# Work of a later layer moved from the setup of an attention stage into its first eleven steps

## Chip, cores and metric

One core of a Trainium2 chip runs the whole program. The metric is the device time in microseconds, the median of several executions.

## What is computed

Two decoder layers on `x` of 8 x 256 tokens by 256 features, in float32. Layer 0: attention with 16 heads of 128, cross attention with linear feature maps to a context of 8 x 64 tokens, and a gated feed-forward part whose weights are first rounded to a 4-bit table (NF4) in blocks of 64. Layer 1: an attention over features, a gated cross attention to the same context ("memory"), and a feed-forward part with ternary weights. Cut to the parts that the change touches:

```python
x = x + attn(layernorm(x), w_qkv, w_o)             # 16 heads, causal mask absent
# values are scaled by the column sums of the softmax: out = einsum('bhqk,bhkd->bhkd', probs, v)
k = (memory_tokens @ wk.T); v = (memory_tokens @ wv.T)   # layer 1, memory: keys and values of the context
scalers_1 = max(abs(blocks), axis=1)               # NF4: one maximum for each block of 64 weights
# the scalers are centred by their mean, rounded to 8 bits per group of 32, and put back
w1 = ternary_quantize(c_fc); w2 = ternary_quantize(c_proj)   # scale = mean(abs(w))
```

## The kernel before

`attention_part` runs the first attention and, beside it, prepares everything of the later parts that depends on weights or on the context alone. `streams_part` then runs the rest over the eight sequences; the change does not touch it.

**Setup.** SyncE issues the loads in program order. TensorE transposes the normalised tokens (16 tiles, `transpose_tokens`), makes the keys and values of the context for layer 0 (`keys`, line 952, and line 1005), and the keys for layer 1 into banks 6 and 7 (`keys(bank[6:8], wk1, ...)`, copied by ACT at line 520). Then a loop over t = 0 to 15 mixes, on TensorE, the transposes of tile t + 4, at even t a feature product (`key_features`, line 967), at t = 4, 8, 12 and at the end a sum of features and values (`key_values`, line 989, "kv sum"), and at t = 1, 5, 9, 13 the memory values of layer 1 (`memory_values`, line 978, copied by ACT at line 545). VectorE in the same loop makes the statistics of four tiles at t = 1 and 5, normalises tile t + 6, splits tile t + 4 into two halves of 16 bits (`xn_lo`, line 676), evicts the feature product (line 728), and at t = 4, 6, 8 takes a third of the block maxima (`block_max`, line 693). At t = 15 it takes their reciprocal (line 736). TensorE then makes the first product of value and output weights (`value_out(0)`), waits for ACT's copy of the last kv sum, and starts the steps.

**Steps.** There are 64 steps, four for each head, each on two sequences: 11 written out, then a loop of eight steps six times, then the last ones. In step i TensorE computes queries and keys of step i (lines 74 to 76), the scores of step i - 1 (line 1064), the update of step i - 2 and its column sums (lines 1091 and 1093). The scores have one pair of banks, so those of step i - 1 wait until ACT has made the exponentials of step i - 2 (line 580); these wait for VectorE's row maximum (line 853). The column sums wait for VectorE's reciprocals (lines 840, 842), which POOL splits. `m_ps` is bank 6, used by `value_out` for each head at the step i = 4, 8, ... (`later_head(i, c, 0)`).

Behind its work for a step VectorE does one-time work, in the order of the code: `block_sums` at i = 0, `scale_codes` (12 instructions in a chain, lines 745 to 768) at i = 2, sums of the ternary weights (line 892) at i = 3 and 4, lin maxima at i = 1, maxima of kv0 (line 906) at i = 5, the ternary scales at i = 6, `linear_scales` at i = 9. At i = 2, 6, 10 it makes the scales of the next head (`scales`, lines 633 to 646) ahead of the row maximum. At i = 10 it waits for `rep_in`, the block scales repeated by column.

**SyncE's queue** is written out by hand; a wait in it holds back all that follows. `absmax_to_all` sends the maxima of a head's weights through memory to all partitions (write, wait, read), `load_prepared` waits for the split of an earlier head and loads a head's weights. The block maxima go out in five small transfers (line 389) and come back by rows (line 391) for `block_sums`.

## Time and profile before

| | |
|---|---|
| median of 3 runs | 932.9 us (932.67 to 932.92) |
| profiled execution, its own time | 934.24 us |
| its span (first to last instruction) | 932.4 us |
| TensorE busy | 858.7 us (92%) |
| VectorE busy | 729.2 us (78%) |
| ACT busy | 520.5 us (56%) |
| POOL busy | 369.0 us (40%) |
| mean granted TensorE clock | 0.98 |

PE is TensorE, PEld its weight loads, DVE VectorE, SPq the queue of SyncE. The granted clock is a share of 2.4 GHz; 0.50 is its lower level of 1.2 GHz. A row of the timeline gives start and length in us, the engine, the line, the operation, the tile written and those read, the shape, how many instructions are merged, and in brackets the idle time before and what ended it. Busy shares are means over stages with different limits, so the stages are read one by one.

### The profile page before, as it was taken

The numbers are of one execution on the slowest core, as the hardware profiler recorded it, in microseconds if no ns is written. First come the engines' busy times: TensorE is split into PE (matmuls) and PEld (weight loads), VectorE is DVE, ScalarE is ACT, GpSimd is POOL, SyncE is SP. The second block draws the span as 40 slices with busy tenths as digits, with TensorE's granted clock in tenths as the row PEclk, the third lists the DMA queues.
The fourth block names the chain that finished last, engine by engine and source line by source line (L and its number), as shares of the span: only waits on it lengthen the run. The fifth ranks groups of instructions, "written<-read, shape, count | busy, mean of one in ns | idle before, by whom it ended". The sixth has DMA issues, their size and how long they took to land. (4 is left out here: it accounts for less than half of the span.)

```text
span 932.4 us, 18697 instructions
## 1 busy us (share of the span) xinstructions
PE 858.7 (92%) x6868; PEld 637.5 (68%) x6868; DVE 729.2 (78%) x1777; ACT 520.5 (56%) x1245; POOL 369.0 (40%) x356
## 2 busy tenths in 40 slices
PE   4798998999999999999999986999988889999786
PEld 3455766777777777777777765787856568777554
DVE  5738867878888788887887745898798879887895
ACT  1435576656665566656665643554364863535556
POOL 3104455545555555545554553044133031522410
PEclk9889999999999999999999997999999999999999
DMA  9022331011101111011100000000000010000001
GB/s 285 32 65 68 55 93 35 2 35 34 34 7 27 34 34 34 0 34 34 34 5 6 1 1 1 1 2 1 1 2 1 1 46 2 1 1 1 1 1 46
DMA packets 34722, 25.56 MB, mean 27 GB/s; under 512 B 9492, under 2 KB 31596, under 8 KB 34668
## 3 DMA queue, kind: packets, MB, share of 16 engines
q1 hardware_dynamic: 34380, 24.56, 10.1%
q8 instruction: 35, 0.57, 0.3%
q10 hardware_dynamic: 288, 0.26, 0.1%
q14 instruction: 19, 0.16, 0.1%
HBM read 22.65 MB, written 2.17 MB: 27 GB/s over the span
## 5 line engine op out<-in xcount | busy, mean ns | idle before, releaser
L476 POOL CAST exp_hi<-exp_scores 128x1024 f16<-128x1024 f32 x64 | 67.0, 1047 | 217.9 <-ACT exp_scores L580 217.9
L74 PE MATMUL banks<-value_out_hi,xn_t_hi 128*128 128x256 f16 x512 | 140.8, 275 | 2.3 <-DVE X L874 2.3
L478 POOL TENSOR_TENSOR exp_lo<-exp_scores,exp_hi 128x1024 f16<-128x1024 f32 x64 | 140.7, 2198 | 5.1
L580 ACT ACTIVATE exp_scores<-banks,exp_bias,unscale 128x256 f32<-128x256 f32 x256 | 141.0, 560 | 2.1
L75 PE MATMUL banks<-value_out_lo,xn_t_hi 128*128 128x256 f16 x512 | 140.6, 275 | 0.0
L76 PE MATMUL banks<-value_out_hi,xn_t_lo 128*128 128x256 f16 x512 | 140.6, 275 | 0.0
L1064 PE MATMUL banks<-qk 128*128 128x256 f32 x512 | 122.7, 383 | 9.9 <-ACT exp_scores L580 9.9
L1064 PEld LDWEIGHTS banks<-qk 128*128 128x128 f32 x512 | 97.2, 191 | 31.4 <-issue 10.5
L874 DVE SCALAR_TENSOR_TENSOR X<-banks,colsum,X 128x256 f32<-128x256 f32 x256 | 106.2, 477 | 11.0 <-DVE colsum L865 9.6
L562 ACT ACTIVATE qk<-banks 128x512 f32<-128x512 f32 x128 | 75.8, 601 | 59.1 <-PE banks L76 59.1
L853 DVE TENSOR_REDUCE neg_rowmax<-banks 128x4 f32<-128x1024 f32 x64 | 78.1, 1221 | 31.4 <-PE banks L1064 31.4
L74 PE MATMUL banks<-xn_t_hi,head_weights_hi 128*128 128x512 f16 x256 | 96.9, 378 | 0.6 <-issue 0.6
L76 PE MATMUL banks<-xn_t_hi,head_weights_lo 128*128 128x512 f16 x256 | 97.0, 379 | 0.0
L75 PE MATMUL banks<-xn_t_lo,head_weights_hi 128*128 128x512 f16 x256 | 96.9, 379 | 0.0
L1282 POOL TENSOR_TENSOR rstd_stream<-rstd_stream,neg_half 128x2 f32<-128x2 f32 x40 | 29.2, 732 | 150.4 <-DVE rstd_stream L1430 139.2
L576 ACT ACTIVATE exp_bias<-neg_rowmax,unscale 128x4 f32<-128x4 f32 x64 | 18.8, 294 | 101.8 <-DVE neg_rowmax L853 101.8
L75 PEld LDWEIGHTS banks<-value_out_lo,xn_t_hi 128*128 128x128 f16 x512 | 50.5, 99 | 12.3 <-issue 0.3
L74 PEld LDWEIGHTS banks<-value_out_hi,xn_t_hi 128*128 128x128 f16 x512 | 50.5, 99 | 11.4 <-DVE X L874 4.4
L76 PEld LDWEIGHTS banks<-value_out_hi,xn_t_lo 128*128 128x128 f16 x512 | 50.5, 99 | 6.2
L1293 POOL TENSOR_TENSOR big_stream<-big_stream,den_stream 128x1024 f32<-128x1024 f32 x16 | 30.3, 1901 | 61.2 <-DVE den_stream L1546 61.2
L435 POOL TENSOR_TENSOR head_weights_lo<-head_weights,head_weights_hi 128x512 f16<-128x512 f32 x32 | 38.7, 1212 | 32.1 <-ACT head_weights_hi L494 32.1
L580 ACT ACTIVATION_READ_ACCUMULATOR exp_scores<-banks,exp_bias,unscale 128x1 f32 x256 | 50.8, 198 | 0.0
(238 smaller groups left out, 1965.9 us busy)
## 6 DMA issues: line engine op xcount, KB each, us to landing
head_weights<-in_wqkv_d SPq DMA_DIRECT2D x32, 128.0 KB, 3.7
weight_absmax_rows<-across_partitions SPq DMA_DIRECT2D x15, 256.0 KB, 4.1
X<-in_x_d SPq DMA_DIRECT2D x4, 512.0 KB, 7.5
head_weights<-in_wqkvt_d SPq DMA_DIRECT2D x16, 128.0 KB, 3.4
head_weights<-in_w_o_d SPq DMA_DIRECT2D x16, 128.0 KB, 3.5
out<-X SPq DMA_DIRECT2D x8, 256.0 KB, 2.1
res_then_ternary_then_kv<-in_c_fc_d SPq DMA_DIRECT2D x1, 1024.0 KB, 6.5
res_then_ternary_then_kv<-in_c_proj_d SPq DMA_DIRECT2D x1, 1024.0 KB, 8.2
```

The source lines that it names most:

```text
L74: nc.tensor.matmul(out, lhs[0], rhs[0], start=first, stop=False)
L75: nc.tensor.matmul(out, lhs[0], rhs[1], start=False, stop=False)
L76: return nc.tensor.matmul(out, lhs[1], rhs[0], start=False, stop=last)
L435: nc.gpsimd.tensor_tensor(wlo[:, u, 2 * a:2 * a + 2], wst[:, u, 2 * a:2 * a + 2], whi[:, u, 2 * a:2 * a + 2], ALU.subtract).then_inc(wlo_r ...
L476: nc.gpsimd.tensor_copy(probh[:, s1_.par], prob[:, s1_.par]).then_inc(exph_ready, 1)
L478: nc.gpsimd.tensor_tensor(probl[:, s1_.par], prob[:, s1_.par], probh[:, s1_.par], ALU.subtract).then_inc(expl_ready, 1)
L562: nc.scalar.activation(qk[:, st.par, s, :], qk_ps[s], ACT.Copy).then_inc(qk_ready, 1)
L580: last = nc.scalar.activation(prob[:, s1_.par, t, :], sc_ps[t // ST][:, t % ST, :], ACT.Exp, bias=nbias[:, t:t + 1], scale=unscale[:, s1_. ...
L853: nc.vector.tensor_reduce(nmax[:, :], sc_both, AX.X, ALU.max, negate=True).then_inc(nmax_ready, 1)
L874: last = nc.vector.scalar_tensor_tensor(out=g.X[:, TP * s2.p + t, :], in0=xm_ps[t // ST][:, t % ST, :], scalar=csum[:, t:t + 1], in1=g.X[: ...
L1064: last = nc.tensor.matmul(sc_ps[b][:, t, :], qk[:, s1_.par, 0, q], qk[:, s1_.par, 1, kk], start=True, stop=True)
L1293: nc.gpsimd.tensor_tensor(by_head(s), by_head(s), den[s][:, t, :].unsqueeze(2).broadcast_to([P, XH, M]), ALU.mult).then_inc(mem_pn[t], 1)
```

## The change

The keys of the memory layer move from the setup to the start of steps 1 and 2, its values to the start of steps 3, 6, 7 and 10, all in bank 6 and each with its copy on ACT ahead of the copies of queries and keys. The thirds of the block maxima move to VectorE's end of steps 0, 1 and 2, their reciprocal and `block_sums` to the end of step 3 and `scale_codes` to the end of step 5. On SyncE the exchange of head 1's maxima goes ahead of the ternary weights, whose two loads now follow one another and stand before the transfers of the block maxima; the repeated block scales go behind the exchange of head 2, the loads of head 3 and the ternary sums.

```diff
--- before.py
+++ after.py
@@ -308,6 +308,7 @@
 
         return c % NP == k and (not known(i) or i // NP >= 1) and runs(i, 0)
 
+    MEMORY_KEYS, MEMORY_VALUES = (1, 2), (3, 6, 7, 10)
     SUM_ABS, TERNARY, ROUNDING = (3, 4), 6, (7, 8)
     LIN_MAX, KV_MAX, LIN_SCALE, KV_HI = 1, 5, 9, FIRST + ROUNDS * BODY
     view = lambda a: a.rearrange("(k p) n -> p k n", p=P)
@@ -368,6 +369,10 @@
         for dst, src in g.early_loads:
             sp.dma_start(dst, src).then_inc(early_loaded, 16)
         load_prepared(2, 0)
+        absmax_to_all(1, 2)
+        sp.wait_ge(kv_ready, NP)
+        for n, (name, kt) in enumerate((("c_fc_d", KT), ("c_proj_d", F2T))):
+            sp.dma_start(tf[n].rearrange("p (k n) -> p k n", k=kt), view(g.dram[name])).then_inc(loads_t, 16)
 
         def by_column(t, flat):
 
@@ -390,28 +395,23 @@
         sp.wait_ge(s1_out, 16 * 5)
         sp.dma_start(s1[:, :, :], by_super(g.scratch[0])).then_inc(s1_in, 16)
 
-        sp.wait_ge(kv_ready, NP)
-        sp.dma_start(tf[0].rearrange("p (k n) -> p k n", k=KT), view(g.dram["c_fc_d"])).then_inc(loads_t, 16)
-        absmax_to_all(1, 2)
         sp.wait_ge(nsum_ready, 2)
         sp.dma_start(spread(2, RB, 3), srow[:, :]).then_inc(nsum_out, 16)
         sp.dma_start(spread(3, P, 2), smax[:, :]).then_inc(nsum_out, 16)
         sp.wait_ge(nsum_out, 32)
         sp.dma_start(srows[:, :, :].rearrange("p q s -> p (q s)"), gathered(2, RB, 3)).then_inc(nsum_in, 16)
         sp.dma_start(mrows[:, :, :].rearrange("p q s -> p (q s)"), gathered(3, P, 2)).then_inc(nsum_in, 16)
-        sp.dma_start(tf[1].rearrange("p (k n) -> p k n", k=F2T), view(g.dram["c_proj_d"])).then_inc(loads_t, 16)
-        sp.wait_ge(nf, NF_REP)
-        sp.dma_start(by_super(g.scratch[1]), rep[:, :, :]).then_inc(rep_out, 16)
-        sp.wait_ge(rep_out, 16)
-        for mine, flat in by_column(repeat, g.scratch[1]):
-            sp.dma_start(mine, flat).then_inc(rep_in, 16)
-
         absmax_to_all(0, 3)
         load_prepared(3, 1)
         sp.wait_ge(tsum_ready, 2)
         sp.dma_start(spread(4, P, 2), tsum[:, :]).then_inc(tsum_out, 16)
         sp.wait_ge(tsum_out, 16)
         sp.dma_start(trows[:, :, :].rearrange("p q s -> p (q s)"), gathered(4, P, 2)).then_inc(tsum_in, 16)
+        sp.wait_ge(nf, NF_REP)
+        sp.dma_start(by_super(g.scratch[1]), rep[:, :, :]).then_inc(rep_out, 16)
+        sp.wait_ge(rep_out, 16)
+        for mine, flat in by_column(repeat, g.scratch[1]):
+            sp.dma_start(mine, flat).then_inc(rep_in, 16)
         sp.wait_ge(lin_max_ready, 5)
         sp.dma_start(spread(5, P, 5), lin_max[:, :]).then_inc(lin_max_out, 16)
         sp.wait_ge(lin_max_out, 16)
@@ -515,9 +515,19 @@
             nc.scalar.activation(k0t[:, m, :], bank[2 + m], ACT.Identity, bias=bk0[:, m:m + 1]).then_inc(k0_ready, 1)
         token_half(2)
         token_half(3)
-        for m in range(KT):
+
+        def memory_keys(m):
             act.wait_ge(k1_full, m + 1)
-            nc.scalar.activation(g.k1t[:, m, :], bank[6 + m], ACT.Copy, scale=float(XD) ** -0.5).then_inc(k1_ready, 1)
+            nc.scalar.activation(g.k1t[:, m, :], m_ps, ACT.Copy, scale=float(XD) ** -0.5).then_inc(k1_ready, 1)
+
+        def memory_values(q):
+            act.wait_ge(v1_full, q + 1)
+            for a in range(2):
+                rows = slice(a * M, (a + 1) * M)
+                last = nc.scalar.activation(
+                    g.v1[rows, 2 * q:2 * q + 2, :, a, 0:XD].rearrange("p b j e -> p (b j) e"),
+                    m_ps[rows, 0:D].rearrange("p (j e) -> p j e", e=XD), ACT.Copy)
+            last.then_inc(v1_ready, 1)
 
         def key_values(q):
             act.wait_ge(kv_full, q + 1)
@@ -536,16 +546,6 @@
                 token_half(t + TP)
             if t % 4 == 0 and t > 0:
                 key_values(t // 4 - 1)
-            if t % 4 == 1:
-
-                q = t // 4
-                act.wait_ge(v1_full, q + 1)
-                for a in range(2):
-                    rows = slice(a * M, (a + 1) * M)
-                    last = nc.scalar.activation(
-                        g.v1[rows, 2 * q:2 * q + 2, :, a, 0:XD].rearrange("p b j e -> p (b j) e"),
-                        bank[6 + q % 2][rows, 0:D].rearrange("p (j e) -> p j e", e=XD), ACT.Copy)
-                last.then_inc(v1_ready, 1)
             if t in (0, 2):
                 act.wait_ge(w_loaded[0], 64)
                 act.wait_ge(wscale_ready, 1)
@@ -556,6 +556,10 @@
 
         def step(i, c, h, nth, r):
             st = Step(i, c)
+            if known(i) and i in MEMORY_KEYS:
+                memory_keys(MEMORY_KEYS.index(i))
+            if known(i) and i in MEMORY_VALUES:
+                memory_values(MEMORY_VALUES.index(i))
             if runs(i, 0):
                 for s in range(2):
                     act.wait_ge(qk_full, i * 2 + s + 1)
@@ -727,13 +731,6 @@
                 dve.wait_ge(kp_full, n + 1)
                 nc.vector.tensor_scalar(kp[:, n // KT, n % KT, :], bank[2 + n % 2], 0.0, keep0[:, n // KT:n // KT + 1],
                                         ALU.max, ALU.mult).then_inc(kp_ready, 1)
-            if t in (4, 6, 8):
-                dve.wait_ge(loads_n, 80)
-                block_max(t // 2 - 2)
-            if t == NT - 1:
-                dve.wait_ge(cleared, 2)
-                dve.wait_ge(block_max_ready, 3)
-                nc.vector.reciprocal(divide[:, 0:BLOCKS], s1t[:, :]).then_inc(divide_ready, 1)
         dve.wait_ge(mhi_ready, 1)
         value_out_lo(0)
 
@@ -877,9 +874,15 @@
                 last.then_inc(x_added, 1)
             if not known(i):
                 return
-            if i == 0:
+            if i < 3:
+                dve.wait_ge(loads_n, 80)
+                block_max(i)
+            if i == 3:
+                dve.wait_ge(cleared, 2)
+                dve.wait_ge(block_max_ready, 3)
+                nc.vector.reciprocal(divide[:, 0:BLOCKS], s1t[:, :]).then_inc(divide_ready, 1)
                 block_sums()
-            if i == 2:
+            if i == 5:
                 scale_codes()
             if i == FIRST - 1:
 
@@ -967,15 +970,28 @@
             nc.tensor.matmul(bank[2 + n % 2], k0t[:, n % KT, n // KT * P:(n // KT + 1) * P], bdk[:, :],
                              start=True, stop=True).then_inc(kp_full, 1)
 
+        def memory_keys(m):
+            if m == 0:
+                pe.wait_ge(mlo_ready, 1)
+                pe.wait_ge(loads, 16 * LOADS)
+            else:
+                pe.wait_ge(k1_ready, m)
+            for k in range(KT):
+                last = nc.tensor.matmul(m_ps, wk1[:, k, m * P:(m + 1) * P], ctxt[:, k, :], start=k == 0, stop=k == KT - 1)
+            last.then_inc(k1_full, 1)
+
         def memory_values(q):
 
-            if q >= 2:
-                pe.wait_ge(v1_ready, q - 1)
+            if q == 0:
+                pe.wait_ge(k1_ready, KT)
+            else:
+                pe.wait_ge(v1_ready, q)
+                pe.wait_ge(mlo_ready, MEMORY_VALUES[q] // NP + 1)
             own = wv1[:, :, :].rearrange("p k (j a e) -> p k a j e", a=2, e=XD)
             for b in range(2 * q, 2 * q + 2):
                 for a in range(2):
                     for k in range(KT):
-                        last = nc.tensor.matmul(bank[6 + q % 2][a * M:(a + 1) * M, b % 2 * P:(b % 2 + 1) * P]
+                        last = nc.tensor.matmul(m_ps[a * M:(a + 1) * M, b % 2 * P:(b % 2 + 1) * P]
                                                 .rearrange("p (j e) -> p j e", e=XD),
                                                 ctxt[:, k, b * M:(b + 1) * M], own[:, k, a], start=k == 0, stop=k == KT - 1)
             last.then_inc(v1_full, 1)
@@ -1006,10 +1022,8 @@
                                         wv0[:, k, :], start=k == 0, stop=k == KT - 1)
             last.then_inc(v0_full, 1)
         pe.wait_ge(loads, 16 * LOADS)
-        keys(bank[6:8], wk1, k1_full)
         pe.wait_ge(cleared, 4)
         pe.wait_ge(k0_ready, KT)
-        pe.wait_ge(k1_ready, KT)
         for t in range(NT):
             if t + TP < NT:
                 transpose_tokens(t + TP)
@@ -1019,8 +1033,6 @@
                 key_values(t // 4 - 1)
             if t % 2 == 0:
                 key_features(t // 2)
-            if t % 4 == 1:
-                memory_values(t // 4)
         key_values(NP - 1)
 
         def value_out(u):
@@ -1032,13 +1044,16 @@
             last.then_inc(m_full, 1)
 
         pe.wait_ge(wlo_ready, 2)
-        pe.wait_ge(v1_ready, NP)
         value_out(0)
         pe.wait_ge(xnl_ready, NT)
         pe.wait_ge(kv_ready, NP)
 
         def step(i, c, h, nth, r):
             st, s1_, s2 = Step(i, c), Step(i, c - 1), Step(i, c - 2)
+            if known(i) and i in MEMORY_KEYS:
+                memory_keys(MEMORY_KEYS.index(i))
+            if known(i) and i in MEMORY_VALUES:
+                memory_values(MEMORY_VALUES.index(i))
             if runs(i, 0):
 
                 if st.p == 0:
@@ -1096,6 +1111,8 @@
             if later_head(i, c, 0):
                 pe.wait_ge(wlo_ready, h * 2 + 2)
                 pe.wait_ge(mlo_ready, h)
+                if known(i):
+                    pe.wait_ge(v1_ready, sum(j < i for j in MEMORY_VALUES))
                 value_out(st.u)
 
         run(pe, step)
```

## Rows read from the trace of the kernel before

**Rows 1.** Windows: PE, PEld, DVE, ACT, POOL busy us (count), granted clock, DMA.
```profile
31.90:37.90 6.00, 5.87 (x22) 4.43 (x22) 1.66 (x5) 1.37 (x9) 0.00 (x0) 0.50 0.01 3
44.90:52.20 7.30, 7.30 (x39) 5.50 (x39) 5.34 (x9) 1.92 (x11) 0.07 (x1) 0.55 0.27 73
63.30:153.60 90.30, 81.57 (x605) 56.70 (x606) 68.65 (x156) 54.86 (x137) 40.85 (x34) 0.99 0.27 68
```
**Rows 2.** Timeline of TensorE, setup: start, us, line, tiles, idle before.
```profile
21.18 3.60 PE L952 MATMUL banks<-ctx_t,wk_t 128*128 128x512 f32 x8
25.62 0.41 PE L960 MATMUL banks<-ident,xn 128*128 128x128 f32 x2 [0.84 <-issue]
...
27.04 1.15 PE L978 MATMUL banks<-wv_t,ctx_t 128*64 128x128 f32 x16
...
32.03 3.65 PE L989 MATMUL banks<-v_aug,res_then_ternary_then_kv 128*128 128x68 f32 x16 [0.31 <-DVE res_then_ternary_then_kv L728]
35.47 2.01 PE L967 MATMUL banks<-feature_k,k_t 128*128 128x512 f32 x2
...
44.67 2.89 PE L989 MATMUL banks<-v_aug,res_then_ternary_then_kv 128*128 128x68 f32 x16 [0.22 <-DVE res_then_ternary_then_kv L728]
...
49.73 2.03 PE L978 MATMUL banks<-wv_t,ctx_t 128*64 128x128 f32 x16
...
60.04 2.00 PE L989 MATMUL banks<-v_aug,res_then_ternary_then_kv 128*128 128x68 f32 x16 [0.84 <-DVE res_then_ternary_then_kv L728]
...
63.32 0.38 PE L74 MATMUL banks<-xn_t_hi,head_weights_hi 128*128 128x512 f16 x1 [0.63 <-issue]
```
**Rows 3.** Timeline of VectorE in the setup.
```profile
26.49 0.42 DVE L676 TENSOR_TENSOR xn_t_lo<-banks,xn_t_hi 128x256 f16<-128x256 f32 x1 [0.79 <-ACT xn_t_hi L502]
...
38.20 1.61 DVE L693 TENSOR_REDUCE nf_s_by_column<-nf_table 128x22 bf16<-128x1408 bf16 x1
...
49.41 0.75 DVE L728 TENSOR_SCALAR res_then_ternary_then_kv<-banks,keep 128x512 f32<-128x512 f32 x1 [1.96 <-PE banks L967]
```
**Rows 4.** Timeline of TensorE in the first steps: scores after a wait.
```profile
74.45 1.97 PE L1064 MATMUL banks<-qk 128*128 128x256 f32 x8 [1.48 <-ACT exp_scores L580]
...
82.42 1.97 PE L1064 MATMUL banks<-qk 128*128 128x256 f32 x8 [0.39 <-ACT exp_scores L580]
...
92.32 1.97 PE L1064 MATMUL banks<-qk 128*128 128x256 f32 x8 [1.53 <-ACT exp_scores L580]
...
116.00 1.97 PE L1064 MATMUL banks<-qk 128*128 128x256 f32 x8 [0.78 <-ACT exp_scores L580]
...
125.18 1.97 PE L1064 MATMUL banks<-qk 128*128 128x256 f32 x8 [1.53 <-ACT exp_scores L580]
...
150.64 3.08 PE L1064 MATMUL banks<-qk 128*128 128x256 f32 x8 [2.24 <-ACT exp_scores L580]
```
**Rows 5.** Timeline of VectorE in the first steps.
```profile
75.60 2.14 DVE L636 TENSOR_SCALAR weight_absmax_all<-weight_absmax_all 128x4 f32<-128x4 f32 x1
...
81.55 0.41 DVE L743 TENSOR_REDUCE nf_max<-nf_max_rows 128x2 f32<-128x256 f32 x1
...
86.87 0.25 DVE L768 TENSOR_TENSOR nf_rep<-nf_q,nf_mean 88x96 bf16<-88x96 bf16 x1
...
91.56 2.28 DVE L892 TENSOR_REDUCE ternary_sum<-res_then_ternary_then_kv 128x1 f32<-128x2048 f32 x1
...
105.31 0.22 DVE L862 TENSOR_SCALAR colsum_raw<-banks,unscale 128x4 f32<-128x4 f32 x1 [1.71 <-PE banks L1093]
...
107.46 2.55 DVE L906 TENSOR_REDUCE lin_max<-kv 128x1 f32<-128x2048 f32 x2
...
111.77 1.21 DVE L853 TENSOR_REDUCE neg_rowmax<-banks 128x4 f32<-128x1024 f32 x1
```
**Rows 6.** Timeline of SyncE's transfers (issue): the block maxima.
```profile
51.71 2.80 SPq L389 DMA_DIRECT2D block_scales<-nf_s_by_column  x5
59.12 0.36 SPq L391 DMA_DIRECT2D nf_s<-block_scales  x1
```

## Prediction

> **What bounds the kernel now.** I read the busy times by stage first, then the order of work on TensorE, on VectorE and on SyncE. The setup ends when the queries and keys of step 0 start, at 63.32 us [rows 2]. From there to the end of step 10 TensorE is busy 81.6 of 90.3 us [rows 1]: the steps are paced by TensorE. Most of its 8.7 idle us lie in front of the scores of steps 2, 3, 4, 7, 8 and 11 (each step computes the scores of the one before it), each released by ACT's exponentials: 1.48, 0.39, 1.53, 0.78, 1.53, 2.24 us [rows 4]. The exponentials wait for VectorE's row maxima, so these are places where VectorE had too much to do. After step 1 it does scales; at the end of step 2 `scale_codes` keeps it from 81.55 to about 87.1 [rows 5]; at the end of step 5 the maxima of kv0 take 2.55 us, then come the head's scales, and the row maximum starts at 111.77, right behind them [rows 5]; scores follow at 116.00 [rows 4], 4.2 us later. VectorE is continuously busy there from 105.31 on, when it last waited for TensorE.
>
> The setup is a different regime: TensorE and VectorE hand work to each other (transposes, feature products, kv sums), and TensorE's granted clock is at the lower of its two levels (0.50, 1.2 GHz) in one stretch and nearly all of another [rows 1]. Before both, TensorE had paused for VectorE repeatedly.
>
> **The setup, step by step.** (1) The memory keys leave: 3.60 us of TensorE, and its next transposes start at 25.62 behind ACT's copy [rows 2]. VectorE cannot use this in full: it is free for `xn_lo(4)` at 25.70, since it waited 0.79 us until 26.49 [rows 3]. Gain so far 0.8, not 4. With POOL's reciprocal root (it follows the statistics) the third eviction of features, which ended just before `block_max(0)` and so started at about 37.5 [rows 3], comes at about 36.6 if kv sum 0 and the feature product stay on the lower clock as they did (3.65 and 2.01 us [rows 2]).
> (2) `block_max(0)`, 1.6 us, stood before statistics that the next transposes wait for: gain now 2.4, so kv sum 1 starts at 42.2 in place of 44.67. There the old one was partly at the full clock (2.89 us); all at the lower it is 3.65, so 0.7 is given back: the eviction of 49.41 [rows 3] comes at about 47.6, gain 1.8. `block_max(1)` lay under VectorE's wait of 1.96 us for TensorE and is worth nothing; `block_max(2)` lies beside a memory value product.
> (3) The memory values of t = 9 cost TensorE 2.03 us at the lower clock [rows 2], those of t = 13, at the full clock, about 1.1 (as at 27.04); both are in TensorE's chain between evictions: gain 1.8 + 2.0 + 1.1 = 4.9. Those of t = 1 and 5 lie beside VectorE work. The reciprocal for `divide` (about 0.6) is beside kv sum 3. I take 5.0: kv sum 3 at 55.0 in place of 60.04, and the queries 3.3 us later, at 58.3 in place of 63.32 [rows 2].
> Bounds: a kv sum is 2.00 us at the full clock [rows 2] against 3.65, a feature product about 1.0 against 2.01. If the last two sums and two products also run low, 2 x 1.65 + 2 x 0.95 = 5.2 is given back and the gain is about 0. If sums 0 and 1 with their products run full, it is 5.0 + 2.6 + 2.6, say 9.5.
>
> **The steps.** All times here are on the old axis, as if the queries started at 63.32 again.
> (4) Memory keys at steps 1 and 2: 1.8 us of TensorE each (half of 3.60). The first is paid in full: step 0's scores move 1.8 later. The second falls into the old wait of 1.48 before 74.45; those scores come at 76.5. Memory values at step 3, 1.15 us at the full clock (the row at 27.04 [rows 2]), push the queries on, less the old wait: step 2's scores at 85.0 (old 82.42). All moved products here make 4.75 us. Before them stand only waits that are met earlier (value_out_lo done, ACT's copies of 0.6 to 0.8 us), and ACT idles there; on its queue the copies of queries come just behind.
> (5) VectorE gets a block maximum of 1.6 us at the end of steps 0, 1, 2. The first lies in its idle wait for scores, the second takes the lin maxima 1.6 later, hidden by the 1.8 of (4); the third replaces `scale_codes` (5.5 us). So row maximum 2 waits for its scores alone, and the scores of 92.32 [rows 4] come at 92.4. The idle 4.7 us of these steps (the three waits above and shorter ones) swallow the 4.75.
> (6) End of step 3: `block_sums` now needs five small writes and a read back. Before, their issue began at 51.71, right after the third block maximum, and the read was issued at 59.12 [rows 6], 7.4 us later, with no other load in flight; with some 2 us to land that is 9.4 to 10 us. The third maximum now ends at 85.2, so the sums are in at about 95.0, while VectorE is free at 92.7. It waits 2.3, then sums, then 2.28 us for the ternary sum [rows 5]: reciprocals at 97.6. TensorE's column sums, which I put at 96.8 by its own work (scores, then products, some 4.4 us after 92.4), need them through POOL: 98.1. Loss 1.3 (0 if the read lands by 93.7; 2.5 if 1.2 later).
> (7) Memory values at step 6: 1.1 us in front of queries 6, covered by VectorE's backlog below.
> (8) `scale_codes` now stands at the end of step 5, directly before the 2.55 us of kv0 maxima, the reciprocals, the scales of head 2 and the row maximum. VectorE arrives 1.4 late from (6), at 106.7; the chain that took 105.31 to 111.77 [rows 5] grows from 6.5 to 6.5 + 5.2 = 11.7 us, row maximum at 118.4, scores of step 6 at 118.4 + 4.2 = 122.6 in place of 116.00: 6.6 late. There is no cover: VectorE was already the bound there. The 5.2 is 5.5 less some of its two long rows: an instruction of 0.17 us that takes 2.14 us while POOL is on exp_lo (the row at 75.60 [rows 5]) shows what is mixed into such chains, so 3.5 to 6. The memory values of steps 6 and 7 lie under this, with all else TensorE has; so does its next wait, of 1.53 before 125.18: VectorE is continuous up to it, so scores come at about 131.8. From there TensorE paces again and carries 6.6 on.
> (9) Memory values at step 10 (1.1) fit into the wait of 2.24 before 150.64 [rows 4]: 0.
> (10) SyncE: moving the absmax exchange ahead of the 1 MB load only frees it sooner; I take no gain, since VectorE comes to the scales of head 1 only behind the reciprocals that wait for ACT. Both loads then run while no other transfer is due before 85. The exchange for head 2, behind `block_sums` now, is issued at about 100 and due at 116; head 3's weights land before step 7; the repeat transfer starts after `scale_codes` at 114 and is due at the end of step 10. All 0; without that slack each would cost its own 3 to 4 us.
>
> Sum: -5.0 + 6.6 = +1.6 us. As a part of (9), the lower clock seen at 143 to 161 might not come when the pause is shorter: the scores at 150.64 take 3.08 us in place of 1.97 [rows 4], so about 1 could come back; I take a tenth of this. Against the profiled span of 932.4 this gives 933.9; the execution's own time is 934.24, its span plus 1.8 at the ends, and the median of the three runs is 932.9, so I add the sum to the median: 934.4.
>
> **Rivals.**
> A. *The setup gain is larger (faster).* One mechanism: with VectorE's pieces gone TensorE's work in the setup meets the full clock in kv sums 0 and 1. Then -9.5 + 6.6 = -3, 930.0. It decides from a setup gain over 8.5. Against it: TensorE pauses longer there than before (22.7 to 26.3), and both old low stretches followed such pauses [rows 1, 2].
> B. *`scale_codes` hides.* If row maximum 5 does not wait for it, the loop costs only (6), 1.4 + 1.1: -5.0 + 2.5, 930.4. The order of instructions on VectorE speaks against it; only a shorter `scale_codes` (3.5) helps: then 932.6.
> C. *The clock eats the setup gain (slower).* The products removed were what kept TensorE working between its waits; with kv sums 2 and 3 on 1.2 GHz the gain is about 0 and the queries may start low too: +6.6, 939.5; half of it, 937.
> The Trainium skill, TensorE: Matmul & The Clock Gate, section "HAM oscillation — how this bites in real kernels", says that pauses between short bursts bring the lower clock back, time after time, so that the same products take double; it speaks against a change that thins out TensorE's setup. The trace agrees as far as its two stretches at 0.50 and 0.55 go, and by that rule alone the time would be rival C's.
> D. *No effect*, gain and loss both small: setup gain 3, loop +3.5 as under B's short chain: 933.4.
>
> **Chances.** Forecast (934.4, own range 932.5 to 936.5) 0.42; A 0.14; B 0.13; C 0.18; D 0.13. Measured runs agree within 0.3 us, but about 0.2% (1.9 us) is what can be told from no change. The forecast's case lies across that border, 0.20 to 0.22; with C slower is 0.38; D and part of the forecast make 0.35; A and B 0.27. The range takes in A and most of C: 929.5 to 939.
>
> **What would show it.** Queries of step 0 at 58 (57 to 59 right, 62 rival C, 54 rival A); granted clock between 25 and 55; a wait of VectorE for a DMA of about 2 us before `block_sums`; scores of step 6 59.3 us behind step 0's queries (old 52.7) and TensorE idle by 2 us twice in steps 6 and 7; row maxima there right behind the scales. It is wrong if scores 6 come less than 56 us behind the queries (B), or if the setup ends outside 56 to 60.

## The result, and the profile after

| | before | after |
|---|---|---|
| median of 22 runs each, us | 932.83 | 934.41 |
| range of the runs, us | 929.79 to 934.38 | 931.01 to 938.38 |
| profiled execution, its own time | 934.24 | 933.34 |
| its span | 932.4 | 931.5 |
| queries of step 0 start | 63.32 | 58.72 |
| last product of the steps' scores starts | 551.9 | 552.7 |

The medians differ by 1.6 us, where +1.6 was summed. The means, 932.4 and 934.7, differ by 2.3 us, a ratio of 1.0025 with a 95% interval of 1.0013 to 1.0036: the changed kernel is slower, by 1.2 to 3.4 us.

The two profiled executions lie the other way round: 933.34 after is 0.9 us less than 934.24 before. The first part of the work, up to the last scores, is 0.8 us longer in them. What follows takes 380.5 us before and 378.8 after; the change does not touch it, and over the profiles of all kernels here it takes 378.8 to 380.9. The profiled execution of before is 1.4 us over its median and has a mean granted clock of 0.980, which only 4 of the 97 executions of that kernel in the groups below have (the others 0.981 to 0.985, but for two of 1026 and 1123 us at 0.84 and 0.75, which are left out everywhere); that of after is 1.1 us under its median. So the traces show where time goes within one execution each, and a difference of 1 or 2 us between two of them need not be the change's.

**The setup after.** Windows: busy us (count) of TensorE, its weight loads, VectorE, ACT and POOL, then the granted clock, the DMA share and GB/s.

```profile
25.00:28.00 3.00, 1.41 (x4) 0.82 (x4) 2.97 (x9) 0.68 (x3) 0.00 (x0) 0.61 0.30 101
28.00:32.00 4.00, 3.04 (x9) 1.29 (x8) 3.82 (x15) 1.89 (x5) 1.01 (x1) 0.50 0.00 0
32.00:36.00 4.00, 4.00 (x16) 3.44 (x17) 0.49 (x2) 0.97 (x8) 0.00 (x0) 0.50 0.00 0
36.00:40.00 4.00, 3.35 (x7) 1.19 (x5) 3.14 (x13) 0.93 (x4) 0.55 (x1) 0.59 0.00 0
40.00:44.00 4.00, 2.43 (x13) 1.96 (x13) 3.55 (x8) 0.77 (x2) 2.74 (x3) 0.84 0.05 12
44.00:48.00 4.00, 4.00 (x14) 2.86 (x14) 0.27 (x1) 1.13 (x8) 0.00 (x0) 0.50 0.47 123
58.70:149.00 90.30, 84.54 (x656) 59.38 (x657) 68.23 (x150) 51.95 (x131) 36.88 (x31) 0.98 0.30 68
```
The lower level (0.50) now holds from 28 to 36 and from 44 to 48, and begins earlier: the same grid before the change reads 1.00 in 25:28 and 0.99 in 28:32. In the 90.3 us from the queries on, TensorE is busy 84.5 us, against 81.6 in a stretch of the same length before [rows 1]: the moved products are here.

The timeline of TensorE in the setup, after (start, us, line, tiles, idle before and what ended it):

```profile
26.59 0.69 PE L963 MATMUL banks<-ident,xn 128*128 128x128 f32 x2 [3.67 <-DVE xn L675]
...
31.33 3.65 PE L1005 MATMUL banks<-v_aug,res_then_ternary_then_kv 128*128 128x68 f32 x16
...
42.44 3.45 PE L1005 MATMUL banks<-v_aug,res_then_ternary_then_kv 128*128 128x68 f32 x16 [0.22 <-DVE res_then_ternary_then_kv L732]
...
50.81 2.00 PE L1005 MATMUL banks<-v_aug,res_then_ternary_then_kv 128*128 128x68 f32 x16 [0.62 <-DVE res_then_ternary_then_kv L732]
...
55.43 2.00 PE L1005 MATMUL banks<-v_aug,res_then_ternary_then_kv 128*128 128x68 f32 x16 [0.84 <-DVE res_then_ternary_then_kv L732]
...
58.72 0.38 PE L74 MATMUL banks<-xn_t_hi,head_weights_hi 128*128 128x512 f16 x1 [0.63 <-issue]
```
The four kv sums start at 31.33, 42.44, 50.81 and 55.43; before they were at 32.03, 44.67, 54.15 (a row not shown) and 60.04 [rows 2]. TensorE waits 3.67 us for VectorE at 26.59, where the memory keys used to stand.

**The steps after.** VectorE, then SyncE's queue:

```profile
78.66 1.61 DVE L697 TENSOR_REDUCE nf_s_by_column<-nf_table 128x22 bf16<-128x1408 bf16 x1
...
91.55 0.25 DVE L702 TENSOR_REDUCE nf_row_sum<-nf_s 88x3 f32<-88x96 bf16 x1 [3.79 <-DMA nf_s<-block_scales]
...
91.85 2.27 DVE L895 TENSOR_REDUCE ternary_sum<-res_then_ternary_then_kv 128x1 f32<-128x2048 f32 x1
...
105.34 0.41 DVE L740 TENSOR_REDUCE nf_max<-nf_max_rows 128x2 f32<-128x256 f32 x1
...
106.21 1.45 DVE L744 TENSOR_SCALAR nf_mean<-nf_sum 88x3 bf16<-88x3 f32 x1
...
109.79 0.25 DVE L765 TENSOR_TENSOR nf_rep<-nf_q,nf_mean 88x96 bf16<-88x96 bf16 x1
109.96 2.56 DVE L909 TENSOR_REDUCE lin_max<-kv 128x1 f32<-128x2048 f32 x2
...
114.28 1.22 DVE L850 TENSOR_REDUCE neg_rowmax<-banks 128x4 f32<-128x1024 f32 x1
```
```profile
80.29 2.78 SPq L394 DMA_DIRECT2D block_scales<-nf_s_by_column  x5
88.44 0.36 SPq L396 DMA_DIRECT2D nf_s<-block_scales  x1
```
The five small writes are issued as the third maximum ends and the read 8.15 us later (before 7.4 [rows 6]); the sums start 3.11 us after the read's issue. VectorE waits 3.79 us for them, and the ternary sum of 2.27 stands behind. Two steps later `scale_codes` runs from 105.34 to 110.0, 4.7 us, then without a gap the maxima of kv0, the scales of head 2 and the row maximum at 114.28. Before, that row maximum was at 111.77 [rows 5], with the queries 4.6 us later than now.

TensorE in the same steps, and the windows:

```profile
94.61 0.18 PE L1106 MATMUL banks<-rowsum_inverse_halves,exp_hi 128*128 128x2 f16 x1 [2.62 <-POOL rowsum_inverse_halves L481]
...
113.02 0.18 PE L1106 MATMUL banks<-rowsum_inverse_halves,exp_hi 128*128 128x2 f16 x1 [1.74 <-POOL rowsum_inverse_halves L481]
...
115.93 0.63 PE L74 MATMUL banks<-xn_t_hi,head_weights_hi 128*128 128x512 f16 x1
...
118.81 1.89 PE L1079 MATMUL banks<-qk 128*128 128x256 f32 x8
...
153.16 1.99 PE L1079 MATMUL banks<-qk 128*128 128x256 f32 x8 [1.41 <-ACT exp_scores L584]
```
```profile
110.00:120.00 10.00, 8.26 (x62) 4.99 (x61) 9.67 (x27) 5.62 (x16) 2.75 (x4) 0.83 0.34 42
...
150.00:160.00 10.00, 8.59 (x67) 5.79 (x65) 8.10 (x18) 9.90 (x26) 6.39 (x5) 1.00 0.10 29
```
Both late points show as waits for VectorE's reciprocals (through POOL): 2.62 and 1.74 us. Behind the second the granted clock is 0.50 from about 114.3 to 117.9: a query product takes 0.63 us, where it takes 0.38 at step 0. Before step 10's scores the wait is 1.41 in place of 2.24, and the scores take 1.99 us in place of 3.08 [rows 4].

All kernels are compared below by the starts of the scores, counted from step 0's queries:

| scores of step | 0 | 3 | 4 | 6 | 9 | 10 | 11 |
|---|---|---|---|---|---|---|---|
| before | 5.2 | 29.0 | 37.1 | 52.7 | 77.3 | 87.3 | 96.4 |
| after | 6.9 | 28.8 | 39.5 | 60.1 | 85.5 | 94.4 | 101.9 |
| late by | 1.7 | -0.2 | 2.4 | 7.4 | 8.2 | 7.1 | 5.5 |

So, in the profiled pair: 4.6 won in the setup, 2.4 lost at the small transfers, 5.0 at `scale_codes`, 0.8 behind it, and 2.7 given back at steps 10 and 11; 5.5 less 4.6 is about the 0.8 us by which the last scores are late.

### The profile page after: what moved, and what is told of

The parts are those of the page before. It is cut to its first block and busy times, and to the rows that moved or that the text cites. A ratio compares the mean times of both kernels' runs of the same rounds, so it can differ in the third digit from the quotient of the medians.

```text
span 931.5 us, 18700 instructions
## 1 busy us (share of the span) xinstructions
PE 858.5 (92%) x6868; PEld 636.4 (68%) x6868; DVE 728.3 (78%) x1777; ACT 520.3 (56%) x1245; POOL 369.7 (40%) x356
## 5 line engine op out<-in xcount | busy, mean ns | idle before, releaser
L1079 PEld LDWEIGHTS banks<-qk 128*128 128x128 f32 x512 | 96.8, 190 | 25.0 <-issue 4.8
L566 ACT ACTIVATE qk<-banks 128x512 f32<-128x512 f32 x128 | 75.8, 600 | 57.5 <-PE banks L76 57.5
```

What stands on the lines that cost most here:

```text
L566: nc.scalar.activation(qk[:, st.par, s, :], qk_ps[s], ACT.Copy).then_inc(qk_ready, 1)
L1079: last = nc.tensor.matmul(sc_ps[b][:, t, :], qk[:, s1_.par, 0, q], qk[:, s1_.par, 1, kk], start=True, stop=True)
```

## The experiments

Four kernels, then four, then three, each group on one chip with the kernel before beside it. The clock is the mean over the runs of a kernel. "Queries" (their start), "scores 6" (the start of step 6's scores, counted from the queries) and "last scores" (the start of their last product) are of its one profiled execution. no_scale and no_mem leave work out and do not compute the right result; all others do.

| kernel | median us | against before, 95% | mean clock | queries | scores 6 | last scores |
|---|---|---|---|---|---|---|
| before (first group) | 932.91 | | 0.983 | 63.32 | 52.7 | 551.9 |
| after | 934.41 | 1.0025 [1.0013, 1.0036] | 0.977 | 58.72 | 60.1 | 552.7 |
| mem_only | 935.95 | 1.0040 [1.0023, 1.0057] | 0.975 | 65.79 | 56.8 | 556.8 |
| nf_only | 932.78 | 1.0003 [0.9987, 1.0019] | 0.984 | 59.10 | 56.8 | 550.1 |
| no_scale | 929.81 | 0.9972 [0.9959, 0.9985] | 0.979 | 58.28 | 57.9 | 550.5 |
| no_mem | 935.33 | 1.0020 [1.0003, 1.0038] | 0.976 | 59.61 | 61.7 | 555.5 |
| early_max | 931.06 | 0.9990 [0.9975, 1.0005] | 0.979 | 59.14 | 57.2 | 550.2 |
| scale_late | 934.30 | 1.0020 [1.0008, 1.0031] | 0.978 | 59.00 | 58.2 | 555.1 |
| best | 933.17 | 1.0010 [0.9999, 1.0022] | 0.979 | 58.47 | 55.0 | 551.7 |
| best_nf | 931.91 | 0.9994 [0.9983, 1.0006] | 0.984 | 60.70 | 52.9 | 550.5 |
| warm | 934.70 | 1.0028 [1.0018, 1.0037] | 0.981 | 59.66 | 59.1 | 553.0 |
| early_split | 931.44 | 1.0000 [0.9990, 1.0010] | 0.979 | 58.68 | 55.5 | 550.1 |
| nf_split | 931.81 | 0.9992 [0.9982, 1.0002] | 0.984 | 59.12 | 53.3 | 550.0 |

The kernel before had medians of 931.94 and 932.01 beside the second and third group, so a kernel of those groups is set against its own kernel before: the changed kernel is 1.6 us over its own.

### The two halves of the change: mem_only and nf_only

mem_only is the changed kernel with the block maxima, sums, quantization and SyncE's order as before; nf_only is the kernel before with those four as changed:

```diff
 # mem_only, against the changed kernel
+            if t in (4, 6, 8):
+                dve.wait_ge(loads_n, 80)
+                block_max(t // 2 - 2)
...
-            if i < 3:
-                dve.wait_ge(loads_n, 80)
-                block_max(i)
-            if i == 3:
...
+            if i == 0:
                 block_sums()
-            if i == 5:
+            if i == 2:
                 scale_codes()
```


> The changed kernel with the NF4 work and SyncE's order put back as before, so that only the memory keys and values are moved. Theory 1 (the setup gives 4 to 5 us, `scale_codes` in front of row maximum 5 takes them back): queries of step 0 at 59.5 to 60.5 (before 63.3), scores of step 6 about 54.5 us behind them (before 52.7, changed kernel 60.1), since VectorE's chain of the first steps moves by the first 1.8 us of keys; in all -1 to -2 us against before. Theory 2 (the steps are paced by TensorE, so the 8 us of products moved there cost most of themselves): scores of step 6 about 59 us behind, in all +2.

> The kernel before with only the NF4 work and SyncE's order of the changed kernel; memory keys and values stay in the setup. Theory 1: queries of step 0 at about 61.8, scores of step 6 about 57.5 us behind them, in all +3 us against before. Theory 2: scores of step 6 53 us behind, in all -1.5.

mem_only started its queries not at 59.5 to 60.5 but at 65.79, later than before, and its scores of step 6 came 56.8 us behind them, between the two theories (54.5 and 59). Its windows and kv sums:

```profile
41.00:50.00 9.00, 7.36 (x26) 5.45 (x27) 6.11 (x11) 1.96 (x11) 3.29 (x3) 0.50 0.22 60
...
56.00:65.00 9.00, 8.15 (x27) 5.36 (x27) 1.98 (x3) 1.59 (x12) 0.00 (x0) 0.50 0.02 2
```
```profile
53.49 2.98 PE L1007 MATMUL banks<-v_aug,res_then_ternary_then_kv 128*128 128x68 f32 x16 [0.55 <-DVE res_then_ternary_then_kv L733]
...
60.82 3.68 PE L1007 MATMUL banks<-v_aug,res_then_ternary_then_kv 128*128 128x68 f32 x16 [0.84 <-DVE res_then_ternary_then_kv L733]
```
All four sums take 3 to 3.7 us. This is what rival C described, in this kernel. The profiled execution (939.51 us, clock 0.971) is one of four of its 12 runs at that clock, all over 939; the other eight are at 0.976 to 0.979 and 932.4 to 936.5, so such a setup is not every execution's. The median of 935.95 is still 3.0 above before, worse than both theories had it (-1 to -2, +2). nf_only, with every memory product in the setup, started its queries at 59.10:

```profile
38.00:41.00 3.00, 3.00 (x20) 2.45 (x20) 2.88 (x12) 1.24 (x4) 0.65 (x1) 0.54 0.00 0
41.00:58.00 17.00, 14.20 (x104) 9.95 (x103) 7.61 (x15) 6.13 (x28) 2.64 (x3) 1.00 0.11 31
```
```profile
43.34 2.00 PE L987 MATMUL banks<-v_aug,res_then_ternary_then_kv 128*128 128x68 f32 x16 [0.22 <-DVE res_then_ternary_then_kv L727]
...
49.93 2.00 PE L987 MATMUL banks<-v_aug,res_then_ternary_then_kv 128*128 128x68 f32 x16 [0.93 <-DVE res_then_ternary_then_kv L727]
```
So moving the block maxima alone starts the queries 4.2 us sooner than the profiled execution of before, where the prediction gave them about 1 (its step 2: 2.4 less the 0.8 of the keys, less 0.7). Most of that goes with the clock: it is full from 41 on, all later sums take 2.00, and from kv sum 1 to kv sum 2 it is 6.6 us with all products in place, against 9.5 before, where the clock was low in that stretch. How much of it a typical execution of before already has can't be told from one profile. Its scores of step 6 came at 56.8, near the 57.5 expected; there it waits 2.33 us and then has the lower clock, scores of 3.65 us. The median is level with before, where the theories had +3 and -1.5.

### What the moved work costs in the steps: no_scale and no_mem

no_scale leaves out the chain of `scale_codes` behind its first reduction and writes ones as block scales. no_mem computes the keys and values of the memory layer nowhere.

```diff
 # no_scale
-            chain(nc.vector.tensor_reduce(sall[:, :], srows[:, :, :].rearrange("p q s -> p s q"), AX.X, ALU.add))
...
+            nc.vector.memset(rep[:, :, :], 1.0).then_inc(nf, NF_REP)
 # no_mem
-    MEMORY_KEYS, MEMORY_VALUES = (1, 2), (3, 6, 7, 10)
+    MEMORY_KEYS, MEMORY_VALUES = (), ()
```


> The changed kernel with 11 of the 12 instructions of `scale_codes` left out (the block scales are then all ones, so the 4-bit weights are wrong). Theory 1: 4.6 us of VectorE vanish from its chain behind step 5; TensorE then limits the scores of step 6 to about 3.6 us earlier and VectorE those of step 7 to 4.6 earlier: in all -4.6 us against the changed kernel. Theory 2: less than 1 us.

> The changed kernel with the memory keys and values not computed anywhere (the memory layer's output is wrong; their copies on ACT are gone as well). Theory 1: 1.8 us less than the changed kernel, the first product of keys, which moves the start of VectorE's chain in steps 1 to 3; the rest lies under VectorE's waits. Theory 2: 6 to 8 us less.

no_scale is 4.6 us below the changed kernel's median, which agrees with the price put on `scale_codes` at the end of step 5; its mean clock is 0.979 against 0.977, so a part of it may be clock. (All 12 instructions behind the first reduction are left out, not 11 as the expectation says.) Its profiled execution has scores 6 at 57.9 in place of 60.1, only 2.2 sooner, because it had lost 1.4 us before that, at the scores of step 4 (40.9, not 39.5), to a stretch at 0.50 from 95.6 to 99 that its edit has no part in. From the scores of step 4 to those of step 6 it takes 17.0 us in place of 20.6, the 3.6 expected. no_mem got no faster, 0.9 us above the changed kernel where 1.8 below was expected; the 6 to 8 of the other theory did not come. Its scores of step 3 are 2.3 us sooner (26.5 against 28.8), then VectorE waits longer for the transfer and TensorE for VectorE:

```profile
91.95 0.25 DVE L703 TENSOR_REDUCE nf_row_sum<-nf_s 88x3 f32<-88x96 bf16 x1 [5.53 <-DMA nf_s<-block_scales]
```
```profile
95.01 0.18 PE L1107 MATMUL banks<-rowsum_inverse_halves,exp_hi 128*128 128x2 f16 x1 [4.37 <-POOL rowsum_inverse_halves L482]
```
The write and read of the block maxima set the time there, 7.9 us from issue to issue and another 4.6 until the sums. Around TensorE's pause of 4.37 us the granted clock falls to 0.50, from 93.7 to 100.5, and the scores of step 4 come at 41.5, 2.0 later than in the changed kernel. So the 2.3 us that the products cost up to step 3 are swallowed by that wait in the changed kernel; what they would cost without it, and at a clock that stays full, this run does not show. Its profiled execution (937.92) is also at the upper end of its 12 runs.

### Where the block maxima should stand, and `scale_codes`: early_max, scale_late, best, best_nf

```diff
 # early_max, against the changed kernel
-            if i < 3:
+            if i == 0:
                 dve.wait_ge(loads_n, 80)
-                block_max(i)
+                for n in range(3):
+                    block_max(n)
 # scale_late
-            if i == 5:
+            if i == 7:
                 scale_codes()
+                hidden_scale()
```
`hidden_scale` is the short chain that follows the quantization in the ternary step; the transfer of the repeated scales moves behind the small loads with it. best has the maxima in step 0, the sums at step 2, and the quantization in halves at steps 7 and 8, `hidden_scale` behind the second; best_nf is the same with the memory products in the setup.

> The changed kernel with all three block maxima at the end of step 0, so that their transfers are under way two steps earlier; sums still at step 3, `scale_codes` still at step 5; the setup is untouched. Theory 1 (the wait of 3.8 us for the block maxima's transfer costs TensorE its 2.6 us of idling before the column sums of step 2): no wait of VectorE for a DMA, scores of step 4 about 36.8 us behind the queries of step 0 (changed kernel 39.5), all behind them 2.6 us earlier, in all -2.6 us against the changed kernel. Rival: the wait was covered, since VectorE is late at step 5 anyway: less than 0.5 us.

> The changed kernel with `scale_codes` and the four instructions that need its maxima at the end of step 7, and the transfer of the block scales behind the loads of that time. Theory 1: scores of step 7 about 64 us behind the queries of step 0 (changed kernel 69.0), step 8 gives back about 1 us, in all -4 us against the changed kernel. Rival: the 5 us are paid wherever they stand: 0.

> The changed kernel with the three block maxima at the end of step 0, their sums at the end of step 2, `scale_codes` halved over the ends of steps 7 and 8. Memory products stay in the steps. Theory 1: TensorE sets the pace nearly throughout, scores of step 7 about 62.5 us behind the queries, in all -6 us against the changed kernel if the setup is as there (58.7), less where the setup's clock is lower. Rival (TensorE has the products to carry): -3.

> As the run before it, but with the memory keys and values in the setup, as in the kernel before. Theory 1 with what `mem_only` and `nf_only` showed (the products in the setup keep the granted clock up): queries of step 0 at 59.1 as in `nf_only`, scores of step 7 about 58 us behind them, in all -8 us against the kernel before and some 3 us less than with the memory products in the steps. Rival (moving the products is worth its 4.6 us of setup): not less than the run before it.

early_max did what was expected: scores of step 4 at 36.8 in place of 39.5, and a median 0.9 us under its kernel before, so 2.5 us better than the changed kernel against its own (2.6 expected); it is the lowest of all kernels that compute everything. Its mean clock, too, is 0.979 against 0.977. In VectorE's timeline the sums no longer wait:

```profile
61.43 4.66 DVE L697 TENSOR_REDUCE nf_s_by_column<-nf_table 128x22 bf16<-128x1408 bf16 x3
...
88.11 0.19 DVE L702 TENSOR_REDUCE nf_row_sum<-nf_s 88x3 f32<-88x96 bf16 x1
```
The other three did not: scale_late is 2.4 us over its kernel before, 0.8 worse than the changed kernel (4 better expected), best 1.2 over, 0.4 better (6 expected), best_nf equal to before (8 better expected), though their scores of step 6 are early. best_nf shows why:

```profile
121.59 1.88 DVE L739 TENSOR_SCALAR nf_mean<-nf_sum 88x3 bf16<-88x3 f32 x1
...
129.65 2.23 DVE L760 SCALAR_TENSOR_TENSOR nf_q<-nf_q_rounded,nf_rqf 88x96 bf16<-88x96 f32 x1
...
140.39 1.84 DVE L823 TENSOR_SCALAR lin_max_all<-lin_max_all 128x5 f32<-128x5 f32 x1
```
```profile
149.30 2.96 PE L1071 MATMUL banks<-qk 128*128 128x256 f32 x8 [2.24 <-ACT exp_scores L579]
```
```profile
140.00:150.00 10.00, 7.06 (x58) 4.67 (x57) 8.83 (x28) 6.01 (x16) 4.07 (x4) 1.00 0.00 0
150.00:160.00 10.00, 10.00 (x67) 7.22 (x66) 6.60 (x14) 7.22 (x17) 7.86 (x7) 0.83 0.27 81
```
The quantization meets VectorE's work of step 9 (`linear_scales`) and step 10 (scales of the head). TensorE is busy 7.1 of the 10 us from 140 on, waits 2.24 us, and then the mean granted clock of 150:160 is 0.83. scale_late and best have the same wait (2.24 and 2.23 us), and their scores behind it take 3.12 and 3.67 us. The profiled scale_late (937.46, its slowest run) also has 0.50 from 96.8 to 100, in steps where it is the changed kernel: its scores of step 4 are 1.8 later.

### The clock in the setup, and the split: warm, early_split, nf_split

```diff
 # warm, against the changed kernel, in TensorE's setup loop
+            if t % 4 == 1:
+                for b in range(2 * (t // 4), 2 * (t // 4) + 2):
...
+                            nc.tensor.matmul(cs_ps[a * M:(a + 1) * M, b % 2 * P:(b % 2 + 1) * P]
...
 # early_split, against early_max (nf_split: the same order, memory products in the setup)
             if i == 5:
                 scale_codes()
+            if i == 6:
+                scale_codes_rest()
```


> The changed kernel, and in the setup the 16 x 4 products of the memory values are issued again at their old places (after tiles 1, 5, 9 and 13), into a bank that nobody reads; the memory keys and the useful memory values stay in the steps. Nothing is left out; work is added. Theory 1 (these products keep the granted clock of TensorE up, so the setup is not shorter for their removal): the granted clock is near 1.00 from 41 us on, and the queries of step 0 start at 56.5 to 59.5 us, no later than the 58.72 of the changed kernel; median 932 to 935. Theory 2 (their work was on the path, as the prediction had it with 3.1 us): the queries start at 61 to 62.5 us, and the median is 936 to 938.

> The changed kernel with the three block maxima at the end of step 0 (as in the run before that had 36.8 us at the scores of step 4) and with the quantization of the block scales in two halves, six instructions at the end of step 5 and five at the end of step 6. Nothing is left out. Theory 1 (VectorE's backlog decides, and ends before the linear scales of step 9 if the halves are done by step 6): scores of step 6 at 53.5 to 55 us after step 0's queries instead of 57.2, scores of step 10 behind a wait of 1.41 us at full clock, and a median of 928.5 to 930.5. Theory 2 (what is won in steps 3 to 7 is given back at the waits of steps 9 to 12, whatever the place): scores of step 10 behind a wait of 2.24 us, the next scores 9 us later, and a median of 930.5 to 932.5.

> The same placing of the block maxima, sums and of the two halves of the quantization, but the memory keys and values stay in the setup as in the kernel before. Nothing is left out. Theory 1 (the gain of the change lies in the block maxima alone, and the memory products cost the setup nothing): queries of step 0 at 58.5 to 61 us, scores of step 6 at 50.5 to 53 us after them, median 927.5 to 930. Theory 2 (given back at the waits of steps 9 to 12): wait of 2.24 us before the scores of step 10, next scores 9 us later, median 931 to 933.

warm adds 64 products (four groups of 1.14 us in its trace) to the setup, and its median is 2.7 us over its kernel before, 1.1 us worse than the changed kernel; the queries start 0.9 later, at 59.66, just outside the first theory's 56.5 to 59.5 and far from the 61 to 62.5 of the second; the median is within the first theory's 932 to 935. The mean clock rises from 0.977 to 0.981, and the runs lie closer, 933.3 to 936.7. Its feature products of 38.45 and 48.62 take 1.02 us, where the changed kernel's (37.44, 48.34) take 1.91 and 1.63. The clock still fell at 44 to 47 (0.50), where the first theory had it near 1.00 from 41 on, so the clock pays for this work only in part. From kv sum 2 to kv sum 3, at the full clock in both, warm takes 5.9 us and the changed kernel 4.6: there the products of t = 13 cost 1.3. From sum 1 to sum 2 warm takes 7.9, with the products of t = 9, and the changed kernel 8.4, at a lower clock: there they cost nothing. Against the 3.1 us that the prediction gave to both, their removal won about 1.

The halves hold six of the 12 instructions each. early_split and nf_split ended level (931.44 and 931.81), above the 928.5 to 930.5 and 927.5 to 930 of their first theories and inside the ranges of their second. In nf_split the scores of step 6 are 2.2 us earlier, at 53.3, but it then has the wait of 2.24 us before step 10, as its second theory had it. early_split has 1.41 us there, as its first theory had it, yet no lower median than early_max: step 6's scores come 1.7 sooner, step 7's 0.3 later (66.4 against 66.1), where the second half stands in front of them.

## Why the prediction came out right, and where it did not

**The sum.** In the profiled pair both terms were right to within a microsecond: setup -4.6 (-5.0 predicted), queries at 58.72 (58.3), scores of step 6 7.4 late (6.6) and 60.1 behind the queries (59.3). The no_scale run supports the main term by the median, 4.6 for `scale_codes`. The forecast of 934.4 is the median measured, and that the agreement is so close is luck. Errors of 1 us with opposite signs lie beneath, 2.7 us came back at steps 10 and 11 that the sum did not count, and the same pair of executions ends 0.9 us the other way. That the change costs the median 1.6 us is measured; that its terms are those of the pair is likely and not shown.

**Steps (1) to (3), the setup.** In the changed kernel they came out one by one: kv sum 1 at 42.44 (42.2 predicted) and 3.45 us long, nearly all at the lower clock as (2) had it, kv sum 3 at 55.43 (55.0). The gains do not stand alone, though, which is how (3) priced them (about 1 us for the block maxima, 0.8 for the keys, 3.1 for the values of t = 9 and 13). nf_only won 4.2 with the block maxima alone and mem_only lost 2.5. The weak step is (3), where the products of t = 9 and 13 were taken as time in TensorE's chain at a clock that stays as it was; warm puts 1.3 us on those of t = 13 and nothing on those of t = 9. Over the first 60 us the granted clock is 0.89 before, 0.83 after, 0.94 in nf_only, 0.78 in mem_only and 0.89 in warm: without the maxima it was higher, without the products lower, in one execution each.

**Rival C** had 0.18. Its mechanism is seen, and in the changed kernel its size was wrong: the queries were not late there. Over all runs, the kernels with the memory products in the setup have a mean clock of 0.983 to 0.984, those without 0.975 to 0.979, and warm 0.981. Within the 22 runs of the changed kernel the time goes with the clock (correlation -0.79, 0.66 us for 0.001), and its slowest runs, near 938, are at 0.974. That the setup varies so from run to run is an inference from spans and mean clocks; only one execution of each kernel was profiled.
The Trainium skill, TensorE: Matmul & The Clock Gate, section "HAM oscillation — how this bites in real kernels", warns of bursts with pauses between. mem_only's windows at 0.50 agree with it; the changed kernel's queries at 58.72 show that such a rule gives the direction and not the price.

**Steps (4) and (5)**, right: scores of step 0 1.7 late (1.8), of step 3 level (29.0 before, 28.8 after), the moved products swallowed by old waits and by the place that `scale_codes` had left (no_mem and nf_only, without products in these steps, have the scores of step 3 at 26.5; no_mem had lost that again by step 4).

**Step (6)**, mis-sized: 2.4 us lost at the scores of step 4 in place of 1.3. The mechanism is as told; issue to issue took 8.15 us and not 7.4, and the sums came 3.11 after the read, not 2 to 2.3. early_max, which takes only this wait away, brings 2.7 us at the scores of step 4.

**Steps (7) and (8)**, mechanism right. `scale_codes` took 4.7 us (5.2), since only one of its instructions was long (1.45 us). The row maximum then came at 114.28, against 113.8 predicted once the 4.6 us of the setup are taken off. TensorE was less free than thought: behind its wait of 1.74 us the granted clock of 110:120 is 0.83, so the queries took 4.1 us in place of 2.6 (those of step 0), and the scores show no wait of their own. That cost little: 4.2 us behind the row maximum, as before, would be 118.5, and they start at 118.81. Rival B is refuted: scores 6 at 60.1, not under 56. The scores of step 7 are 7.1 late behind a wait of 1.37, the old 1.53 nearly kept, as (8) had it.

**Step (9)**: the tenth given to a lower clock that does not come is what happened. The wait before step 10's scores shrank to 1.41, the window stayed at 1.00, and 2.7 us of the 8.2 came back at steps 10 and 11, where the prediction counted about 1 at a tenth. The steps have about 3.4 us at 0.50 in both profiles; they only lie elsewhere, at step 6, where the time was hidden. That lowers the profiled execution below the sum and makes room for the larger (6).

**Step (10)**, right: no wait for the moved transfers appears.

Rival A (a setup gain over 8.5) did not come. nf_only, with a full clock from 41 on, gained 4.2 and not 9.5, but its kv sum 0 still ran low in part (2.83 us), so rival A's price of both sums at the full clock was not tested. Rival D (933.4, so +0.5) lies below the interval, which begins at +1.2; its setup gain of 3 and loss of 3.5 were 4.6 and 5.5 in the profiled pair. A slip in the working changes nothing: for a chain of 3.5 us step (8) gives a loss of 4.9, so rival B's second figure would be 932.8 and not 932.6, and rival D's loss of 3.5 would be 4.9. None of the kernels that compute everything is shown to be faster than the kernel before: early_max comes nearest, 0.9990 with an interval that reaches over 1.

## What to carry to other kernels

Before work is moved off an engine's busy stage, look whether the engine really was the bound there: of the filling products between TensorE's waits, one group was on its path here and the others were nearly free, and the kernels without them show a lower mean granted clock. A one-time chain on an engine that is continuously busy cost its full length here (no_scale), and moving it on cost again when it met the next one-time work, so follow the backlog up to the next place where that engine is idle. A round trip through memory that was hidden by a setup stage of other work becomes a wait as soon as its start is moved nearer to its use: start it first, then distribute the rest. And compare medians with medians: one profile of each kernel can differ by more than the change is worth.

## What was not expected of the hardware

The same TensorE products run at either clock level from one kernel to the next, and the spread of the changed kernel's executions (931.0 to 938.4) is 1.6 times that of before, with the mean clock going along (0.974 to 0.982). A pause of 2.24 us before the scores of step 10 was followed by the lower clock in before (scores of 3.08 us), scale_late, best, best_nf and nf_split (2.99 us), but not in nf_only and no_mem, where the next scores come 7.4 us later in place of 9.1; those two had been at the lower clock at step 6, behind a pause of 2.33, and nf_split, with the same pause there, had not. A pause of 1.41 never was followed by it, but pauses of 1.74 (the changed kernel), 1.66 (early_max) and 1.60 us (early_split) before column sums in steps 5 to 7 were, and one of 2.62 in the changed kernel was not. So the length of the last pause does not decide; what does is open.

Single small VectorE instructions that take 0.17 to 0.25 us elsewhere took 1.45 to 2.23 us, and which one it was changed with the chain's place. In the changed kernel the long one, of 1.45 us, ends at 107.66. POOL's work in that moment:

```profile
105.50 2.13 POOL L478 TENSOR_TENSOR exp_lo<-exp_scores,exp_hi 128x1024 f16<-128x1024 f32 x1
```
It ends at 107.63. The other long ones read here, two in before (84.11 and 75.60) and three in best_nf, too end within 0.1 us behind such an instruction of POOL. Why they wait for it no run tests; prices read for one place carry about 1.5 us of this.
